# Banded attention: two banks for the transposed scores, and one more mask product in each step

## The reference

```
q = (x @ Wq + bq) ; k = (x @ Wk + bk) ; v = (x @ Wv + bv)      # 16 heads of 8
scores = einsum('bhid,bhjd->bhij', q, k) * HD ** -0.5
valid = (j <= i) & (j >= i - W + 1)                             # W = 32
scores = where(valid, scores, -inf)
out = einsum('bhij,bhjd->bhid', softmax(scores), v)
return out.transpose(0, 2, 1, 3).reshape(b, s, dim) @ Wo + bo
```

## Time and profile before

| | us |
|---|---|
| median of 3 executions | 1277.04 |
| lowest, highest | 1276.58, 1280.21 |
| the profiled execution | 1281.2 |
| its span | 1279.4 |
| mean granted clock of TensorE | 0.895 |

### The profile page before, as it was taken

How to read it: one execution, slowest core, us unless ns; L and a number is a source line. 1 busy time by engine, 2 the same in 40 slices (tenths; PEclk the granted TensorE clock), 3 DMA queues, 4 the chain that set the end, 5 groups by cost and what they waited for, 6 DMA issues and landing times. The chain is left out here.

```text
span 1279.4 us, 19655 instructions
## 1 busy us (share of the span) xinstructions
PE 1081.6 (85%) x6168; PEld 433.6 (34%) x6168; DVE 954.7 (75%) x2178; ACT 691.3 (54%) x1056; POOL 423.4 (33%) x352
## 2 busy tenths in 40 slices
PE   3376998979899979889989996488863988999998
PEld 1021222222222325434444443133332543444443
DVE  5689998969999557697778775677525769777776
ACT  2011776757777785556656663155421555666665
POOL 3001352252000014555545562000001455555554
PEclk9555999979999999899999998589675999999999
DMA  7311022022100107456755951211111745767662
GB/s 273 88 42 33 2 72 71 19 56 72 34 16 2 39 12 181 126 151 177 189 147 145 236 146 49 76 53 53 28 38 28 177 128 144 188 186 199 189 187 68
DMA packets 72912, 131.72 MB, mean 103 GB/s; under 512 B 13400, under 2 KB 48344, under 8 KB 72808
## 3 DMA queue, kind: packets, MB, share of 16 engines
q1 hardware_dynamic: 71512, 123.94, 36.6%
q10 hardware_dynamic: 1296, 6.49, 1.3%
HBM read 115.08 MB, written 14.91 MB: 102 GB/s over the span
## 5 line engine op out<-in xcount | busy, mean ns | idle before, releaser
L386 DVE TENSOR_REDUCE Aatt_mx<-Aatt_sc 128x1 f32<-128x512 f32 x512 | 318.4, 682 | 25.4 <-PE Aatt_sc L230 16.5
L334 ACT ACTIVATE Aatt_prob<-Aatt_st 128x1024 f32<-128x1024 f32 x256 | 248.4, 1023 | 86.4 <-PE Aatt_st L239 85.2
L230 PE MATMUL Aatt_sc<-ks,qs 48*128 48x512 bf16 x512 | 171.3, 432 | 61.5 <-DVE Aatt_mx L386 26.7
L1708 POOL TENSOR_TENSOR M1ex_low<-M1ex_hid,M1ex_high 128x512 f16<-128x512 f32 x132 | 153.8, 1165 | 149.3 <-PE M1ex_acc L1563 71.3
L1708 POOL TENSOR_TENSOR M2ex_low<-M2ex_hid,M2ex_high 128x512 f16<-128x512 f32 x132 | 153.8, 1165 | 136.4 <-PE M2ex_acc L1563 80.3
L1601 ACT ACTIVATE M1ex_sil<-M1ex_ring,unscale 128x512 f32<-128x512 f32 x132 | 90.7, 687 | 99.1 <-PE M1ex_ring L1546 99.1
L1601 ACT ACTIVATE M2ex_sil<-M2ex_ring,unscale 128x512 f32<-128x512 f32 x132 | 90.7, 687 | 96.8 <-PE M2ex_ring L1546 96.7
L250 PE MATMUL Aatt_pv<-Aatt_prob,vg 128*32 128x512 f32 x1024 | 142.2, 629 | 0.6 <-ACT Aatt_prob L334 0.6
L1645 DVE SCALAR_TENSOR_TENSOR M2ex_ring<-M2ex_ring,unscale,M2ex_sil 128x512 f32<-128x512 f32 x132 | 100.0, 758 | 48.9 <-ACT M2ex_sil L1601 44.7
L1645 DVE SCALAR_TENSOR_TENSOR M1ex_ring<-M1ex_ring,unscale,M1ex_sil 128x512 f32<-128x512 f32 x132 | 99.9, 757 | 48.0 <-ACT M1ex_sil L1601 41.4
L230 PEld LDWEIGHTS Aatt_sc<-ks,qs 48*128 48x128 bf16 x512 | 37.2, 95 | 259.0 <-DVE Aatt_mx L386 231.0
(11 more groups left out here) (420 smaller groups left out, 1847.7 us busy)
## 6 DMA issues: line engine op xcount, KB each, us to landing
M1ex_cb<-comb SPq DMA_DIRECT2D x130, 256.0 KB, 4.0
M2ex_cb<-comb SPq DMA_DIRECT2D x130, 256.0 KB, 4.0
M_wt<-wsplit SPq DMA_DIRECT2D x132, 192.0 KB, 3.9
wsplit<-split_cut SPq DMA_DIRECT2D x9, 704.0 KB, 5.7
qs<-stack SPq DMA_DIRECT2D x32, 96.0 KB
ks<-stack SPq DMA_DIRECT2D x32, 96.0 KB
split_raw<-in_wg_dram ACTq DMA_DIRECT2D x3, 704.0 KB, 7.3
split_raw<-in_wu_dram ACTq DMA_DIRECT2D x3, 704.0 KB, 10.9
```

The lines of the kernel that those rows point to most:

```text
L230: pe.matmul(sc_bank(k, i)[:, :], qs[k][rows, jp, qt * P:(qt + 1) * P], ks[k][rows, jp, h * CH:(h + 1) * CH], start=True, stop=True).then_i ...
L334: act.activation(prob[e % 4][:, :, :].rearrange("p a c -> p (a c)"), st[pr][:, :, :].rearrange("p a c -> p (a c)"), ACT.Exp, scale=SCALE). ...
L386: dve.tensor_reduce(mx[k][:, m, part // 2:part // 2 + 1], sc_bank(k, i)[:, :], AX.X, ALU.max).then_inc(red_done, 1)
L1708: pool.tensor_tensor(low[q % 3][:, :], hid[q % 3][:, :], high[q % 3][:, :], ALU.subtract).then_inc(low_ready, 1)
```

## The change

The transposed scores get two banks, bank pr for pair pr, and FREE_ST becomes 2: a mask product waits for the exponential two before it. The third bank becomes a tile `warm`. Into it each of the 64 steps writes one more product of identity and mask, 320 columns of the whole array, between the transposed scores and the row scores. Nobody reads it and it waits for nothing.

```diff
-    FREE_ST, FREE_SC = 3, 2
+    FREE_ST, FREE_SC = 2, 2
...
-        st = [ps(f"st{i}", [P, W2], F32) for i in range(3)]
+        st = [ps(f"st{i}", [P, W2], F32) for i in range(2)]
+        warm = ps("warm", [P, W2], F32)
...
                     for pr in range(2):
                         e = 2 * s + pr
-                        bank = st[(k + e) % 3]
+                        bank = st[pr]
                         pe.wait_ge(exp_done, n * 2 * STEPS + e + 1)
                         pe.matmul(bank[:, :], env.ident16[:, :], mask_k[:, :], start=True, stop=True)
                     for h in range(2):
                         for pr in range(2):
                             rows = slice(HALF * pr, HALF * pr + KROWS)
-                            bank = st[(k + 2 * s + pr) % 3]
+                            bank = st[pr]
...
                             if h == 1:
                                 mm.then_inc(st_done, 1)
+                    pe.matmul(warm[:, :], env.ident16[:, :], mask_k[:, :], start=True, stop=True)
                     for off, kk, qt in score_blocks(s, k, nxt, nxt2):
                         scores(n + off, kk, qt)
...
-                        act.activation(prob[e % 4][:, :], st[(k + e) % 3][:, :], ACT.Exp,
+                        act.activation(prob[e % 4][:, :], st[pr][:, :], ACT.Exp,
                                        scale=SCALE).then_inc(exp_done, 1)
```

## The result

| | before | changed |
|---|---|---|
| median us | 1276.81 (8 executions) | 1284.51 (8) |
| lowest, highest | 1276.13, 1281.26 | 1280.64, 1289.12 |
| ratio, 95% interval | | 1.005 [1.0031, 1.0068] |
| profiled execution, its span | 1281.2, 1279.4 | 1284.16, 1282.2 |
| banded stage, first mask product to end of last copy | 115.1 | 121.5 |

The change makes the kernel slower, by 7.7 us instead of the 17 forecast. The spans of the two profiles differ by only 2.8 us, because before's profiled execution was later ahead of the stage: its first mask product starts at 825.22 us, that of the changed kernel at 820.49. In the thirteen profiles of this case this start lies between 819.1 and 827.9. Inside the stage the loss is 121.5 - 115.1 = 6.4 us.

A forecast was written before the change was run, and what follows sets the result against it. Banded attention was taken as bound by TensorE at 1.2 GHz and VectorE in full steps at 2.4 GHz. (60 - 7) x 0.31 = 16.4, less 1.1, gave +15.3 on 1281.2: 1296.5, lowered to 1294 us; range 1277 to 1321.

The forecast's parts named there:

- Low step: Banded-attention step at 1.2 GHz, where TensorE waits for nobody: from 1.98 to 2.47 us through the extra product.
- step 0 to 1 of a batch: First step of a batch, without weighing: two banks lengthen it from 1.08 to 1.41 to 1.45 us at 2.4 GHz.
- without row scores: Last batch's steps at 2.4 GHz: 1.47 us against 1.15, from the ring of exponentials with two banks.
- The two gaps: Empty array time on both sides of the extra product, at each change of shape: 2 x 0.11 us low.
- The rival without gaps: Weight loads pulled ahead strike the gaps: low step 2.25 us, clock rises as before and holds, 1275 us; chance 0.08.
- The cover: High steps with row scores: VectorE's wait of 0.40 us hides the product's 0.33, leaving 0.07; step stays 1.58 us.
- Price of the low clock: Banded stage: 0.31 us lost per microsecond at 1.2 GHz above 7, added to -1.1 us for all high after the start.
- The low time: Banded stage: 60 us at 1.2 GHz, a first stretch of about 30 and one later fall of about 30.
- The start of the sum: Profiled execution of 1281.2 us, 4 us above the median; about half taken off, from 1296.5 to 1294.
- The clock's course stays as it was: Rival: low stretches as before, 22 low steps x 0.49 = +10.8, 1289 us in all; chance 0.15.
- Stuck at 1.2 GHz: Rival: the banded stage's low stretch never ends, +41 us, 1320 us; chance 0.15.
- Does what warmth is for: Rival: after one short low start the clock holds, also at batch ends, -1.1 us, 1276 to 1280 us; chance 0.12.

The follow-up runs named there:

- e3_half_rows: The changed kernel with its extra product, in the same place, on 51 of the array's 128 rows, the shape of its neighbours; 1285.03 us, 1.0057 of before.
- e4_double: The changed kernel with a second extra product directly behind the first in each step; 1288.42 us, 1.0085 of before.
- e11_change_again: The changed kernel itself, unaltered, measured once more; 1286.30 us, 1.0053 of before.
- e9_change_kept_high: The changed kernel plus three products ahead of each batch's wait for maxima and four behind each row-score tile ahead of the stage; 1279.47 us, 0.9988 of before.
- e1: The changed kernel without the extra product, so two banks alone; 1282.74 us, 1.0033 of before.
- e6: The kernel before, with three banks, plus the extra product between transposed and row scores, written into the next mask's bank; 1282.78 us, 1.0042 of before.
- e2_head_of_step: The changed kernel with the extra product moved to the head of each step, beside the mask products; 1278.05 us, 0.9997 of before.

## Why the prediction was right, and where it was wrong

**Steps: right.** Low step 2.47 forecast, 2.48 measured; full high step 1.58 and 1.58; step 0 to 1 of a batch 1.41 to 1.45 and 1.41; a high batch 13.69 and 13.69; without row scores 1.47 and 1.47. The two gaps are there, and e3_half_rows, where they are not, shows that the change of shape makes them. The prediction reads the 0.52 us of "issue" in the earlier trace rows as the gap; that is the idle time of the weight loads, and for 0.41 of it the last mask product still streams, so that the gap is the 0.11 of the sum. The Trainium skill ("TensorE: Matmul & The Clock Gate", Step-by-step: what each phase is for) lets a weight load be pulled ahead where the row groups don't conflict or a background buffer takes it. In e4_double a load for all 128 rows came in ahead while a product on the same rows ran (851.81), so a conflict of rows alone does not hold a load back; at a change of shape no load came ahead, and why is not shown. The rival without gaps has fallen.

**The cover: right.** The product costs a full high step nothing, and the 0.07 us left are confirmed by e4_double's 1.65.

**Price of the low clock: right within 1.2 us.** The sum, -1.1 and 0.31 for each microsecond low above 7, gives, with the 35 us of the first profile, +7.6; the stage measured +6.4. With the 10.6 us of e11_change_again it gives 0.0; measured 114.5 - 115.1 = -0.6. Between the two profiles a microsecond low cost 7.0 / 24.4 = 0.29.

**The low time: wrong, and this is the step that failed.** "I take 60 us low: a first stretch of about 30, and one later fall that again lasts about 30." The two profiles have 35 and 10.6, and in the mean clock of whole executions the changed kernel (0.900 in both measurements, 20 executions) is no lower than the kernel before (0.898 to 0.900, 93 executions). The second fall was forecast rightly in number, but the stretches lasted 21.3, 13.7, 7.2 and 3.4 us. Behind it stands "I expect each low stretch to last 20 us and more", which I had drawn from how much of a low step streams: one of four did. Two rose as soon as in the fuller steps of before. Putting 35 in place of 60 takes 7.8 us off the forecast of 1294, to 1286, where the two medians are 1284.5 and 1286.3.

What the runs show in its place: the changed kernel loses with no more low time than before, because the same low time costs more. A low step is 0.50 us longer than before and a full high one is not. An estimate from the profiles: with 23 us low, the mean of its two, the changed stage takes 118.0 us, the mean of 121.5 and 114.5. Before, a microsecond low costs (1.98 - 1.58) / 1.98 = 0.20, so that its stage with 23 us low instead of 41 would take 115.1 - 18 x 0.20 = 111.5. The difference is 6.5 us; the medians differ by 7.7 and 6.8. That a higher clock gives much of it back is what e9_change_kept_high shows.

**The start of the sum: a smaller error.** I left some 2 of the 4 us by which before's profiled execution lay above its median in the sum, in case they came from the long low stretch. That stage started 4.7 us later than in the changed kernel's profile, which speaks for time lost ahead of it, but its 41 us low are also more than the changed kernel's profiles have; where the 4 us lay is not shown.

**Rivals.** "The clock's course stays as it was" was the nearest in its way: in single profiles the course changed, but the mean clock did not. Its 22 low steps x 0.49 and 1289 us were above the 1284.5 measured. "Stuck at 1.2 GHz" did not occur in 20 executions of the changed kernel. "Does what warmth is for" is half true: high, the clock fell once in each profile of the changed kernel, three times before.

**Open:** how long a low stretch lasts in the changed kernel as compared with before. It differs by a factor of six between stretches of one program, and the mean clocks, which show no difference, are of whole executions. Why the stretches did not last is open too. How the loss divides between product and banks is known only within the intervals of e1 and e6.

## What to carry to other kernels

Before adding work to keep a clock up, look at its two neighbours: beside products of its own shape an extra product cost its columns (0.15 us at 2.4 GHz, 0.27 at 1.2), between products of another shape about twice as much (0.33 and 0.50). Put it where the engine idles ahead of the places at which the clock fell, here in the wait at a batch's end: 24 products there gained 0.4%, and 64 in the middle of the steps, together with a bank less, lost 0.5%. Work added to a step is dearest where the clock is low, since nothing covers it there. Where one execution's clock differs from another's, one profile gives the price per microsecond but not the microseconds; forecast those as a range.

## What the runs showed that I had not expected

Two banks alone cost 0.33% [0.15%, 0.51%] without lengthening one full high step, and with a mean clock of 0.894 against 0.900. The same changed program had 35.0 and 10.6 us at 1.2 GHz in two executions. And a product on 51 of 128 rows kept nothing high: 52 us low in its profile and a mean clock of 0.889, with TensorE's low steps as short as those of e2_head_of_step.
